# The causal mask of the second attention moves from a matmul into VectorE's maximum pass, and all engine orders are new

## What is computed

```python
x = layernorm(x + L0_attn(x))          # 16 heads of 64, full softmax ("first attention")
x = layernorm(x + L0_ffn(x))           # routing, small table network
x = layernorm(x + L1_attn(x))          # linear + windowed attention, gate
x = layernorm(x + L1_ffn(x))

def L1_ffn(x, ...):                    # "second attention" and experts
    h = layernorm(x, ln_g, ln_b)
    q = l2norm(h @ Wq) * q_scale; k = l2norm(h @ Wk) * k_scale; v = h @ Wv
    logits = q @ k.T * 10.0
    logits = where(causal, logits, -1e9)
    out = softmax(logits) @ v @ Wo
    h = layernorm(out, ln_g, ln_b)
    gate = softmax(h @ gate_w + gate_b)
    exp_out = gelu(h @ w1[e] + b1[e]) @ w2[e] + b2[e]      # 8 experts, 128 -> 512 -> 128
    return layernorm(sum_e gate[e] * exp_out[e], ln_g, ln_b)
```

## Time and profile before

| | before |
|---|---|
| median of 3 runs | 2387.47 us |
| lowest, highest | 2386.63, 2390.48 us |
| span of the profiled execution (first to last instruction) | 2377.5 us |
| outside the span, by the median | 10.0 us |
| PE busy | 2234.4 us (94% of the span) |
| DVE busy | 1557.1 us (65%) |
| ACT busy | 1348.7 us (57%) |
| POOL busy | 847.3 us (36%) |
| mean granted TensorE clock | 0.986 |

### The profile page before, as it was taken

One profiled execution on the slowest core, in us unless ns is written; L12 is line 12 of the kernel. 1 busy time (PEld: TensorE's weight loads), 2 busy tenths in 40 slices (PEclk: granted clock), 3 DMA queues, 4 the chain that ended last, 5 costly groups with the idle time before them and its releaser, 6 DMA issues.

```text
span 2377.5 us, 44469 instructions
## 1 busy us (share of the span) xinstructions
PE 2234.4 (94%) x16347; PEld 1546.4 (65%) x16347; DVE 1557.1 (65%) x4247; ACT 1348.7 (57%) x3784; POOL 847.3 (36%) x1010
## 2 busy tenths in 40 slices
PE   8999999999999999999999999999999999999897
PEld 5565666856667566676667666676666756667465
DVE  5677676676657766577765867558675676656752
ACT  5346464764547755476545757466564764646452
POOL 3315551064510643116521356114561054510630
PEclk9999999999999999999999999999999999999999
DMA  4000001000010000110001000001001000010001
GB/s 149 28 1 1 1 2 45 10 32 1 1 54 11 23 1 1 54 33 1 1 10 45 32 1 1 27 28 32 1 1 45 10 32 1 1 36 10 32 1 49
DMA packets 24722, 50.46 MB, mean 21 GB/s; under 512 B 3316, under 2 KB 3900, under 8 KB 24252
## 3 DMA queue, kind: packets, MB, share of 16 engines
q1 hardware_dynamic: 24508, 47.63, 6.2%
HBM read 45.52 MB, written 2.10 MB: 20 GB/s over the span
## 4 chain that ended last, share of the span: by engine, by line
PE 77%; DVE 12%; ACT 5%; POOL 4%; issue 2%; DMA 0%; SPq 0%; DVEq 0%; ACTq 0%
PE ps L1494 10%; PE ps L1515 10%; PE ps L651 5%; PE ps L668 5%; PE ps L602 5%; PE ps L868 4%; PE ps L1428 4%; PE ps L906 4%; PE ps L1527 4%; PE ps L1445 4%; PE ps L799 3%; PE ps L782 3%; PE ps L835 2%; PE ps L1383 2%; PE ps L1394 2%; POOL rn L1737 2%
## 5 line engine op out<-in xcount | busy, mean ns | idle before, releaser
L1048 POOL TENSOR_TENSOR rstd<-ve,half_neg 128x4 f32<-128x4 f32 (+1 forms) x56 | 66.8, 1193 | 971.9 <-DVE ve L1029 971.9
L1515 PEld LDWEIGHTS ps<-wbuf,QK 128*128 128x128 f32 x2048 | 266.0, 191 | 108.2 <-issue 99.9
L1304 POOL TENSOR_TENSOR E<-E,ri 128x512 f32<-128x512 f32 x240 | 247.4, 1039 | 180.4 <-DVE ri L1103 180.2
L1618 ACT ACTIVATE QK<-ps,cols 128x512 f32<-128x512 f32 x256 | 172.7, 687 | 209.1 <-PE ps L1494 208.8
L1494 PE MATMUL ps<-h2T,wbuf 128*128 128x512 f32 x512 | 275.4, 626 | 0.2
L1744 POOL TENSOR_TENSOR work<-work,ri 128x128 f32<-128x128 f32 x480 | 231.2, 506 | 120.5 <-DVE ri L1667 119.7
L1515 PE MATMUL ps<-wbuf,QK 128*128 128x128 f32 x2048 | 270.2, 275 | 0.0
L929 ACT ACTIVATE E<-ps,nm 128x256 f32<-128x256 f32 x480 | 225.6, 485 | 64.3 <-DVE nm L1096 64.0
L1578 ACT ACTIVATE work<-ps,nm 128x128 f32<-128x128 f32 x480 | 198.5, 425 | 98.5 <-DVE nm L1658 98.4
L1737 POOL TENSOR_TENSOR rn<-ss,half_neg 128x8 f32<-128x8 f32 x120 | 195.1, 1637 | 156.8 <-DVE ss L1643 155.9
L1096 DVE TENSOR_REDUCE nm<-ps 128x2 f32<-128x512 f32 x256 | 168.8, 684 | 23.4 <-PE ps L651 21.7
(11 more groups left out here) (280 smaller groups left out, 4529.5 us busy)
## 6 DMA issues: line engine op xcount, KB each, us to landing
wbuf<-in_w SPq DMA_DIRECT2D x128, 256.0 KB, 3.2
xT<-in_xT SPq DMA_DIRECT2D x8, 256.0 KB, 3.5
xr<-in_xr SPq DMA_DIRECT2D x8, 256.0 KB, 4.2
bias_t<-in_bias_t SPq DMA_DIRECT2D x1, 2048.0 KB
out_y<-xn SPq DMA_DIRECT2D x8, 256.0 KB, 2.2
wqkv<-in_wqkv SPq DMA_DIRECT2D x1, 1536.0 KB
wo<-in_wo SPq DMA_DIRECT2D x2, 512.0 KB, 7.6
rows<-in_rows SPq DMA_DIRECT2D x1, 531.0 KB, 6.7
```

Source lines behind the costliest of these rows:

```text
L1304: nc.gpsimd.tensor_tensor(L.E[:, g % 4, :, :], L.E[:, g % 4, :, :], L.ri[:, g, :].unsqueeze(2).broadcast_to((P, NT, S)), ALU.mult)\
L1515: last = nc.tensor.matmul(bank2[2 + x % 2][:, t * P:(t + 1) * P], hid[:, x % 2, c, t * P:(t + 1) * P], w2[:, x % WB, c, :], start=(c == 0) ...
```

## The change

The mask matmul is gone, and the score matmuls start their own accumulation. `causal` is now a float32 tile of 256 columns: the first 128 are zero, the last 128 hold 0 or -1e9 as before. On DVE, the two reductions per head pair are replaced by four `tensor_tensor_reduce`, one for each head and query tile. Each adds the mask to the scores, multiplies by -1, writes the result back over the scores in PSUM, and takes the minimum along the row, which is the negated maximum. The built program shows each of them as two instructions, the main one and one that writes the accumulated column. The exponential reads the negated scores with `scale=-1.0`. `max` is signalled once for each head, after its two tiles, where it was signalled once for each pair.

```diff
-        causal = sb("causal", [P, P], BF16)
+        causal = sb("causal", [P, 2 * P])
...
-            nc.gpsimd.affine_select(out=causal[:, :], in_=causal[:, :], compare_op=ALU.is_ge, fill=CAUSAL_FILL,
+            nc.gpsimd.affine_select(out=causal[:, P:2 * P], in_=causal[:, P:2 * P], compare_op=ALU.is_ge, fill=CAUSAL_FILL,
...
+                dve.wait_ge(setup_pool, SETUP_POOL)
...
-                    for i in range(2):
-                        nc.tensor.matmul(tri(L.bank[i][:, 0:384], 3)[:, 0::2, :], ident_bf[:, :],
-                                         causal[:, :].unsqueeze(1).broadcast_to((P, 2, P)),
-                                         start=True, stop=False, skip_group_check=True)
-                yield
-                if u < HP:
...
-                                                    start=False, stop=True, skip_group_check=True)
+                                                    start=True, stop=True, skip_group_check=True)
...
-                        act.wait_ge(sem_of(L, "max"), upto("max" + L.tag, HP * n + u + 1))
+                        act.wait_ge(sem_of(L, "max"), upto("max" + L.tag, NH * n + h + 1))
...
-                                                 accum_out=L.rs[:, h, t:t + 1]).then_inc(sem_of(L, "exp"), 1)
+                                                 scale=-1.0, accum_out=L.rs[:, h, t:t + 1]).then_inc(sem_of(L, "exp"), 1)
...
-                    for t in range(NT):
-                        ins = nc.vector.tensor_reduce(L.nm[:, 2 * u:2 * u + 2, t],
-                                                      ps[:, first_bank:first_bank + 2, t * P:t * P + (t + 1) * P],
-                                                      AX, ALU.max, negate=True)
-                    ins.then_inc(sem_of(L, "max"), 1)
+                    for i in range(2):
+                        for t in range(NT):
+                            o = L.bank[i][:, t * P:t * P + (t + 1) * P]
+                            ins = nc.vector.tensor_tensor_reduce(o, o, causal[:, (1 - t) * P:2 * P], -1.0, 3e38, ALU.add,
+                                                                 ALU.min, L.nm[:, 2 * u + i, t:t + 1])
+                        ins.then_inc(sem_of(L, "max"), 1)
```

Nearly every string of `ORDER` is new too; one line of each stands for them:

```diff
     ("both", "tensor"):
-        "000011111111101100110101110111110110110101111100001100110011110011110010111101010111010011011110"
+        "010011111011011100101101011101110101110110101110010101010100111101010110101101010110010101110001"
```

66 lines of the change are left out of this document (32 added, 34 removed).

## The result

The changed kernel takes 2327.03 us (median of 4 runs, 2326.47 to 2331.51) against 2388.97 us (4 runs, 2386.63 to 2394.95) for the kernel before: ratio 0.9751, 95% interval 0.9728 to 0.9775.

The account below looks back on a forecast made before the run. PE, busy 94% of the span, was taken as the bound, with DVE's free quarter to spend. 28 (mask) - 3.5 (last part) - 7 (late copies) + 14 (order) = 31.5 us gave 2356 us, range 2331 to 2395.

Parts of the forecast that it names:

- the late copies: In the middle parts' second-attention stretches, copies PE waits for come late on fuller DVE: 0.5 us for each of 14, 7 us.
- the lost last part: In the last part's second attention DVE's work doesn't fit, so the 3.5 us saved on PE there are lost.
- the rounds: New order in the rounds of head pairs: only neighbours change, costed at nothing, within 1 us a part either way.
- What PE loses: Mask matmuls between transposes and scores go: 0.22 us for each of 128 head pairs, 28 us; bounds nothing and 49.
- What DVE gains: Four passes with column writes replace two reductions: 1.66 against 1.02 us, 0.65 more a head pair, 83 us over 128.
- the lower end of 0.34: Lowest extra DVE price per head pair: columns alone at the slope plus 0.07 for each of eight instructions, 1.36 us.
- The wait for the maximum gets no longer: ACT's wait before the exponentials: about 0.83 us for one head's two passes, where it waited 1.02 for both heads.
- The end of the attentions: New order where PE waits for the gelu and table loads: 2 us a part saved, 14 us in seven middle parts.
- If the clock's stretches change in number: Sign of being wrong: the stretches at reduced PE clock, one in each middle part before, change in number.
- the first rival: The clock's stretch at the end of the attentions goes and DVE's pass costs 0.34: 49 us, 2338 us; chance 0.22.
- The median of 2387.47 lies 10.0 above: Offset between the profiled execution's span of 2377.5 us and the median time, used to turn span 2346 into 2356 us.
- The second and third: Second: PE waits for DVE, pass 0.9 more, 2377 us, chance 0.15. Third: DVE becomes the bound, 2406 or 2449, 0.13.

Follow-up runs that it names:

- the mask alone: The change's mask passes on DVE and max signal per head, with every engine order of the kernel before: 2356.73 us, ratio 0.9898 to the kernel before.
- the mask twice: The kernel before with the two mask matmuls of each head pair issued again behind themselves: 2407.19 us, ratio 1.0106.
- after: The changed kernel, with the mask on DVE, a max signal per head and new engine orders: 2327.03 us, ratio 0.9751 to the kernel before.
- The orders alone: The new engine orders with the mask matmuls kept on PE directly before the scores and the reductions of the kernel before: 2364.89 us, ratio 0.9928 to that kernel.
- the kernel with the new rounds and the old end: The changed kernel with the old orders from the end of the attentions on in the middle parts: 2346.18 us, ratio 0.9825.
- the kernel with the mask and the new end: Mask on DVE, old orders except from the end of the attentions on in the middle parts, which are new: 2341.44 us, ratio 0.9826.

## Why the prediction was wrong

The direction and the bound were right: PE sets the time, DVE's free quarter pays, and PE's saving a mask is 0.22 us. The size was off by half. Three steps failed: the price of the DVE pass, with the late copies and the lost last part that hang on it (10.5 us charged, nothing of it came), the rounds, put at nothing (8 to 10 us), and the clock, kept as it was (12 to 14 us).

- **What PE loses, 28 us: right.** With the signal the mask alone gives 24 (20 to 28), 29 at one clock, the mask twice costs 25, and a middle part is 16 x 0.21 shorter. Between transposes and scores without a mask the starts lie 0.42 us apart in 49 of the 83 places of the mask alone, as predicted; in after, where only 39 such places are left, it is 0.42 in 7 and 0.48 in 14. PE's busy time fell by 45.1, near the 49.1 of the mask's rows by luck: those count the overlap with their neighbours, the mask takes 3.5 us of busy time from a part, 25 in seven, and the rest is the orders' and the clock's.
- **What DVE gains, 0.65 a head pair: the price failed.** It is 0.27 to 0.29, below the lower end of 0.34. The main instructions start 0.19 to 0.25 and 0.38 to 0.39 apart, near the 0.26 and 0.39 worked out; the column write, put at 0.09 from a reciprocal, costs nothing, and four of them are 0.36 of the 0.43 by which the sum (1.66 against 1.23) was too high. The sum has two slips besides: it compared starts (1.66) with a duration (1.02) where the starts of before are 0.94 apart, and its slope of (680 - 424)/256 gives 128 ns for 128 columns, not 133. DVE's busy time rose by 47.9, not 80 to 110. 256 columns take 465 ns, where a reduction of 256 took 424: no half pace. The half pace that the Trainium skill gives ("Vector Engine (DVE) Microarchitecture Reference", section "Points that are easy to get wrong") is for two sources in SBUF, so by its letter it doesn't speak of scores in PSUM; no run here has both sources in SBUF.
- **Late copies 7 us and the last part's 3.5 us: neither came.** At 85% DVE isn't late, and the last part kept its saving (39.6 to 37.4 with 3.4 us of it at 1.2 GHz, 35.8 without). These two and the pass are one error, 10.5 us: 28 - 10.5 = 17.5 was forecast for the mask on DVE, and 29 came. Where the pass did cost 0.87 (the run with one more reduction), DVE at 92% cost 1.8 us a middle part, near the 0.5 a stretch that I charged at 94%.
- **"The wait for the maximum gets no longer", costed at nothing: the sentence was right and the question beside the point.** ACT's idle time there fell from 98.5 to 66.9 us. Without the signal per head the mask's removal brings 4 us instead of 24 (8 instead of 29 at one clock), and the whole change 19 instead of 59. I asked whether the new pass would lengthen the wait, and not whether the old wait would become the bound once PE's work was gone. The condition under which 28 us could be taken was in the change, but the prediction never named it; that the 28 came right without it was luck.
- **"In the rounds of head pairs the pieces are the same and only neighbours change; I cost that at nothing, within 1 us a part": this step failed too, a term put at nothing without a reason.** With the signal they are worth 1.2 to 1.4 us a part, 8 to 10 us (7 to 9 by the whole times); without it, by the sums above, nothing. 1.1 of it is busy time that PE loses with the same matmuls, so a neighbour does change what a matmul costs. One such price could have been read: behind L667 a mask is dearer. There L667 to L1419 and on to L1425 takes 1.02 + 0.32 us, and L667 to L1422 without a mask 1.01, so 0.32 instead of 0.22, at 21 places where the old order has 7. That is 1.4 us of the 8 to 10; the rest isn't traced to its neighbours.

The orders alone, PE in a middle round:

```profile
597.28 1.08 PE L667 MATMUL ps<-ET,ETw 128*64 128x256 f32 x8
598.30 0.39 PE L1419 MATMUL ps<-causal,ident_bf 128*128 128x256 bf16 x2
598.62 0.93 PE L1425 MATMUL ps<-QK 64*128 64x128 f32 x8
```

- **The end of the attentions, 14 us: 7 to 10 of pace, 17 with the clock.** The steps were worked out rightly. L710 waits no more and starts 4.66 us after the transposes (4.65 forecast, the wait for `fT` included), and the second L1488 comes after 12.3 us in the two parts without a stretch at 1.2 GHz, where 12.75 were forecast, and after 14.0 in the five with one. What was read wrongly is the 15.9 of before: 3.4 us of full-speed time are lost to the clock in it. In the kernel with the new rounds and the old end the same mark lies at 14.6 us in parts with a loss of 1.7, where after has 14.0, so at equal clock the new order brings 0.6 up to there, the 0.5 that the prediction gave for this case, and 1.3 to 1.5 over the whole part.
- **The clock: the forecast kept it as it was,** but for the 0.5 to 3 us in the end's term. After stands at 0.989 and loses 1.7 or nothing instead of 3.4 at the end of the attentions; this is 12 to 14 us, the largest term that was missed. "If the clock's stretches change in number" stands among the prediction's signs of being wrong, and they did: seven of 6.8 us before, five of 3.4 after. The forecast gave no term for it, and the first rival had it.
- **"The median of 2387.47 lies 10.0 above" the span: wrong reading.** The profiled execution of after has a span of 2325.3 and took 2327.11, 1.8 outside it, and that holds for every run. The profiled execution of before was then one of some 2379.3 us, and the median came from others. Of the 29 us between forecast and result, 8 are this; they are part of the clock's 12 to 14, since the profiled execution stood at 0.986. On the spans of the two profiled executions the forecast was 31.5 and the difference 52.2: some 11 of the missing 20.7 are the pass, 8 to 10 the rounds, and the end's 4 to 7 too many are made good by some 6 of the clock (0.986 to 0.989).

Of the rivals, the first had the outcome nearly right (2338) with both of its mechanisms: a cheap pass, and less loss to the clock, which was more than halved and didn't go. It lacked the rounds, and its 3 us a part for the end were 1.3 to 1.5 and the clock, so its time was near partly by luck. The second and third rest on prices that the pass doesn't have.

## What to carry to other kernels

When work is taken off a full engine, look for the loop that stands just behind it, and ask at what grain it is signalled: here the saving on PE was paid out in full only because the maximum was handed over a head at a time. An accumulating instruction's second half can be free in the queue; take its price from starts and not from busy time, and leave room for zero. An order searched for one set of costs is worth something only together with the edits it was searched with, so price the order with them in place, and compare versions at the same granted clock before a few us are put down to an edit.

## What the runs showed of the hardware

- The column write of an accumulating DVE instruction shows 141 ns and starts together with the next instruction (594.97 and 594.97).
- Middle parts with the same instructions, in one execution, lose 0, 1.7, 3.4 or 6.8 us of full-speed time to the clock, and the part gets longer by 1.7, 3.0 and 6.0 (279.1, 280.8, 282.1 and 285.1 us in the kernel with the mask and the new end). Over whole executions 0.001 of the mean clock goes with some 2 us (1.8 over the 35 executions of before).
- The clock fell to 0.66 over 35 us in which PE was busy for 34.77. In these traces a share of busy time this high doesn't tell whether it holds.
- The same matmuls in another order cost PE 1.1 us less busy time in a part (268.2 against 269.3 us at the same loss to the clock).
